# Reordering maxima, projections and the join of the maxima inside an attention group (order lists of one pipelined slot)

## The reference

```
q = split_heads(x @ Wq.T + bq); k = ...; v = ...
q_lr = einsum('bhtd,hdr->bhtr', q, Wq_lsr); k_lr = ...
scores = einsum('bhir,bhjr->bhij', q_lr, k_lr) * scale      # causal mask above the diagonal
attn = softmax(scores, axis=-1)
y = einsum('bhij,bhjd->bhid', attn, v);  out = y @ Wo.T + bo
```

## Time and profile before

| what | us |
|---|---|
| median of 3 runs | 4275.05 (4274.4 to 4277.15) |
| the profiled execution | 4274.05 |
| its span, first to last instruction | 4272.3 |
| PE matmul busy in the span | 3743.8 (88%) |
| DVE, ACT, POOL busy | 2262.9, 1473.4, 687.8 |

### The profile page before, as it was taken

How to read it: one execution, slowest core, us unless ns; L and a number is a source line. 1 busy time by engine, 2 the same in 40 slices (tenths; PEclk the granted TensorE clock), 3 DMA queues, 4 the chain that set the end, 5 groups by cost and what they waited for, 6 DMA issues and landing times. The chain is left out here.

```text
span 4272.3 us, 57451 instructions
## 1 busy us (share of the span) xinstructions
PE 3743.8 (88%) x21481; PEld 2587.1 (61%) x21481; DVE 2262.9 (53%) x3990; ACT 1473.4 (34%) x2753; POOL 687.8 (16%) x859
## 2 busy tenths in 40 slices
PE   5898998998998989989989832799999999999990
PEld 3555555555555555555555422788888888888880
DVE  2565564664664655655646457444454444544445
ACT  1343442443443433434424400333333333333324
POOL 2021121121121211211211210011111111111100
PEclk8999999999999999999999965699999999999995
DMA  4224233133322332242331110333344333443328
GB/s 154 68 81 113 58 102 98 46 97 98 93 70 78 100 102 64 79 117 59 102 97 41 43 57 5 104 117 106 121 127 136 114 108 121 126 136 113 111 69 324
DMA packets 187321, 422.56 MB, mean 99 GB/s; under 512 B 39777, under 2 KB 42849, under 8 KB 178401
## 3 DMA queue, kind: packets, MB, share of 16 engines
q1 hardware_dynamic: 167408, 367.98, 28.7%
q0 software_dynamic: 14336, 34.09, 4.2%
q10 hardware_dynamic: 5376, 17.83, 1.0%
HBM read 245.70 MB, written 72.38 MB: 74 GB/s over the span
## 5 line engine op out<-in xcount | busy, mean ns | idle before, releaser
L841 DVE TENSOR_REDUCE max_slots<-shared_banks 128x1 f32<-128x512 f32 (+3 forms) x1536 | 786.0, 548 | 497.0 <-PE shared_banks L636 370.7
L792 ACT ACTIVATE probs<-scores_t 128x512 f32<-128x512 f32 (+3 forms) x1536 | 671.4, 492 | 661.5 <-PE scores_t L678 653.1
L1510 PE MATMUL m_ps_h<-m_tokens_t,m_w_parts 128*128 128x512 f32 x3072 | 740.0, 391 | 1.6 <-DVE m_tokens_t L1448 1.6
L1510 PE MATMUL m_ps_y<-m_w_parts,m_hidden_parts 128*128 128x512 f32 x3072 | 737.0, 390 | 0.5
L678 PE MATMUL scores_t<-q_operands,k_operands 128*128 128x512 f32 (+3 forms) x1536 | 570.5, 412 | 114.3 <-DMA q_operands<-minus_max 108.3
L1510 PEld LDWEIGHTS m_ps_y<-m_w_parts,m_hidden_parts 128*128 128x128 f32 x3072 | 575.5, 188 | 125.3 <-issue 6.3
L1510 PEld LDWEIGHTS m_ps_h<-m_tokens_t,m_w_parts 128*128 128x128 f32 x3072 | 575.6, 188 | 120.1 <-issue 2.0
L633 PE MATMUL shared_banks<-k_operands,q_operands 96*128 96x512 f32 (+3 forms) x1536 | 555.0, 392 | 13.8 <-DVE natural L834 7.9
L1417 ACT ACTIVATE m_hidden<-m_ps_h,m_b 128x512 f32<-128x512 f32 x256 | 176.6, 690 | 817.8 <-PE m_ps_h L1510 804.6
L678 PEld LDWEIGHTS scores_t<-q_operands,k_operands 128*128 128x128 f32 x1536 | 294.0, 207 | 237.0 <-DMA q_operands<-minus_max 114.9
L633 PEld LDWEIGHTS shared_banks<-k_operands,q_operands 96*128 96x128 f32 x1536 | 314.5, 206 | 193.2 <-issue 138.2
(11 more groups left out here) (202 smaller groups left out, 3139.4 us busy)
## 6 DMA issues: line engine op xcount, KB each, us to landing
m_w_raw<-in_w1T SPq DMA_DIRECT2D x64, 1024.0 KB, 5.1
m_w_raw<-in_w2T SPq DMA_DIRECT2D x64, 1024.0 KB, 7.9
q_operands<-natural SPq DMA_DIRECT2D x384, 128.0 KB, 2.7
k_operands<-natural SPq DMA_DIRECT2D x384, 128.0 KB, 2.7
wqk_group<-scratch_wqk SPq DMA_DIRECT2D x32, 1024.0 KB, 5.2
natural<-in_xT SPq DMA_DIRECT2D x8, 2048.0 KB, 9.1
x_residual<-in_x SPq DMA_DIRECT2D x64, 256.0 KB, 2.7
scratch_x<-probs SPq DMA_DIRECT2D x64, 256.0 KB, 2.0
```

Of the source, the lines that this page charges most:

```text
L792: act.activation(probs[:, slot_of(k, h // 2), h % 2, c0:HALF], st[:, (HG * k + h) % SCORE_BANKS, c0:HALF], ACT.Exp, scale=SCALE).then_inc( ...
L841: dve.tensor_reduce(mx[:, h, slot:slot + 1], src[:, 0:n], AX.X, ALU.max).then_inc(bank_free[bank], 1)
L1510: mm = pe.matmul(bank, a, b, start=(first and n == 0), stop=(final and n == len(pairs) - 1))
```

## The change

Only the lists of the order change. The 48 maxima start behind part 8 instead of part 1 and end behind part 51 instead of part 55. Projections 0 and 1 stand at the parts 46 and 47 (before 47 and 49), projections 2 and 3 at 56 and 57 (before both at 50). The join stands at part 55 (before 58), so that projections 2 and 3 are behind it. The inversions of the first half move from 40, 44, 48, 49 to 30, 42, 45, 45; those of the second half of the group before, in the next slot, from 0, 0, 0, 14 to 0, 4, 4, 5. No instruction is added or taken away.

```diff
-MAX_AFTER = (0, 2, 2, 0, 1, 2, 0, 1, 2, 0, 2, 0, 1, 0, 1, 2, 0, 0, 0, 1,
-             0, 3, 1, 0, 1, 1, 1, 0, 1, 0, 2, 1, 1, 0, 1, 1, 1, 1, 1, 1,
-             0, 3, 0, 1, 0, 1, 1, 1, 1, 1, 0, 1, 1, 0, 1, 1, 0, 0, 0, 0)
-PROJ_AFTER = (47, 49, 50, 50)
-JOIN_AFTER = 58
-INVERT_AFTER = ((40, 44, 48, 49), (0, 0, 0, 14))
+MAX_AFTER = (0, 0, 0, 0, 0, 0, 0, 0, 2, 0, 2, 1, 1, 0, 3, 0, 0, 0, 3, 0,
+             2, 0, 3, 1, 0, 0, 2, 0, 1, 2, 0, 1, 2, 1, 2, 0, 0, 2, 1, 1,
+             0, 2, 2, 4, 1, 0, 1, 2, 1, 0, 1, 1, 0, 0, 0, 0, 0, 0, 0, 0)
+PROJ_AFTER = (46, 47, 56, 57)
+JOIN_AFTER = 55
+INVERT_AFTER = ((30, 42, 45, 45), (0, 4, 4, 5))
```

## The result

| | before | after |
|---|---|---|
| median of 4 runs, us | 4275.18 (4274.4 to 4277.15) | 4247.84 (4245.81 to 4250.01) |
| ratio to before, 95% interval | | 0.9935 [0.9918, 0.9953] |
| profiled span, us | 4272.3 | 4246.9 |
| mean granted clock of the span | 0.924 | 0.930 |

A forecast was written before the change was run, and what follows sets the result against it. PE's waits and clock bound the kernel; 103 + 41 - 35 - 13 - 13 - 36 - 13 - 11 - 7 = 16 us gained from 4274.05 gave 4258. Own range 4235 to 4267; 8 in 10: 4215 to 4310.

The forecast's parts named there:

- wait for the joined maxima: At starts of slots 1 to 3, PE's wait for the join's DMA, hidden by projections 2 and 3: 103 us gained.
- clock behind that wait: At 23 slots the granted clock no longer falls after the wait: 1.8 us each, 41 us gained.
- slot start without maxima: At 23 slot starts, only eight scores in parts 0 to 7, then strips: 1.5 us each, 35 us lost.
- x split, wait and clock: Slot 2, seven batches: PE waits 5.1 us for POOL's late split, 36 us lost; the clock falls, 13 us lost.
- tail and slot 0, with its clock, in batches 1 to 7: Late residual rows in seven tails lose 11 us; slot 0's maxima lose 13 over 8 batches, its fallen clock 13.
- DVE's lag: DVE's reductions, packed into fewer parts, fall behind: 0.3 us for 25 slots, 7 us lost.
- the undisturbed 52.65: Length in us of slot 0 before the change, at full clock, less a 0.52 us wait for an activation table.
- T: The moment PE leaves a slot's last weighing; times at the next slot's start are counted from it.
- the eight maxima: Maxima moved out of parts 0 to 7: done elsewhere they cost 1.7 us a slot, between 0.7 and 2.7.
- clock's rival: Clock falls at ordinary starts of slots 1 and 3 too: 2.5 us for 16 starts, 40 us, 4298; chance 0.30.
- cancelling rival: Maxima cost 2.7 and DVE lags 0.7 us a slot; half of that leaves 4275, no change; chance 0.21.
- hidden split: Slot 2's x split is in time after all: 36 + 13 us come back, with cheaper maxima 4187; chance 0.07.

The follow-up runs named there:

- experiment 2: Changed kernel's parts singly: join and projections with the old maxima order, 4353.83 us, 1.019; maxima and join with the old projections, 4269.66 us, 0.999.
- second kernel of experiment 2: Changed kernel with its maxima, join and inversions, but projections back at 47, 49, 50, 50: 4269.66 us, 0.999.
- experiment 1: POOL splits only 16 tokens of each chunk of the next x: on the changed kernel 4187.27 us, 0.9792; on the kernel before 4273.3 us, 0.9995.
- experiment 3: Changed kernel with slot 0's maxima from part 1, 4241.61 us; or slot 3's projections at 46, 47, 49, 50 and join at 58, 4238.95 us.
- experiment 5: Changed kernel, slot 2 rearranged, DVE subtracting one chunk of x, all projections behind the join: 4202.35 us; with slot 0 and slot 3 edits too, 4191.04 us.
- first kernel: Changed kernel with only slot 2 rearranged: DVE subtracts one chunk of x, inversions at 28 to 36, all projections behind the join: 4202.35 us, 0.983.
- second kernel of experiment 5: Changed kernel with slot 2 rearranged, slot 0's maxima from part 1 and slot 3's projections ahead of its last score: 4191.04 us, 0.9796.

## Why the prediction was right

The direction, the mechanism and the order of the terms held. By its own terms:

| term of the prediction | forecast | measured |
|---|---|---|
| wait for the joined maxima | +103 | +103, gone in all 24 slots |
| clock behind that wait | 23 x 1.8 = +41 | +41; clock 1.00 at all 23 starts |
| slot start without maxima | 23 x 1.5 = -35 | 23 x (53.84 - 52.65) = 23 x 1.2 = -28 |
| x split, wait and clock | 7 x (5.1 + 1.8) = -49 | 7 x (6.3 + 2.3) = -60 |
| tail and slot 0, with its clock, in batches 1 to 7 | -11 - 12 - 13 = -36 | -30 |
| DVE's lag | -7 | no wait seen |

The 41 can be checked in the kernel before: its 22 whole slots 1 to 3 last 54.5 us on average from first score to last weighing, 1.9 more than the undisturbed 52.65, 41 us in all. The last column gives 26, where the spans differ by 25. That it closes is no separate check, since the 28 and the 60 are what is left of whole slots. The forecast of 16 missed by less than its terms suggest: three terms were charged 6 to 7 us too high each, and the split 11 too low, so that a part of the closeness is luck.

One sum of the prediction does not come out. From the bounds of the slot start (23 us either way) and of DVE (7 less, 10 more) the range is 4228 to 4291; the 4267 stated lies 8.5 us under 4275, the least gain that a measurement can tell, and is no bound. The measured 4248 lies in either.

**The join.** The wait went in whole. In the last batch's slot 2, where I had let the joined maxima cost 1.4, PE waits 1.55 us, but for POOL's masks: it is the chain of experiment 2, which I had not seen, and that the two numbers agree is chance. In all slots with projections the projections cover that chain as well, so the sum doesn't show the gap; the second kernel of experiment 2 does, and there my estimate failed by 17 us and more.

**The slot start.** Step 0 was weighed at T + 3.5 (502.64 - 499.14) where 3.8 stood, and the first maximum came at T + 6.0 behind a wait of 0.55, where T + 6.2 and 0.5 stood. Its cost, 1.2 a slot, is what is left of slot 1 against the undisturbed 52.65 worked out from the earlier trace rows; the price of the eight maxima at their new places cannot be read apart from it. I had not foreseen that a few starts wait longer for strips: slot 3 of the batches 4 and 5 lasted 55.1 and 55.5 us, 1.3 and 1.7 more than the others.

**The next sequence's x.** This step was right and undersized: a wait of 6.3 on average, not 5.1. SP's queue and POOL, after the change, batch 1:

```profile
553.28 0.51 SPq L431 DMA_DIRECT2D q_operands<-natural  x1
...
571.09 0.39 SPq L413 DMA_DIRECT2D natural<-in_xT  x1
```

```profile
585.22 9.27 POOL L527 TENSOR_TENSOR x_parts<-natural,x_parts 128x1024 fp32r<-128x1024 f32 x4
```

T is 552.97 here. The strips start at T + 0.3 and not T - 0.2, and from them to the end of the split it is 594.49 - 553.28 = 41.2 us, not 40.1: these make the 6.62 of this slot out of 5.1. PE came to projection 0 at 594.63 - 6.62 = T + 35.0, as forecast (34.8). Wait and clock together, from slot 2's 62.4 against experiment 1's 53.8, are 8.6 a slot and not 6.9; less the 6.3 of the wait, 2.3 are left for the clock where 1.8 stood. That these 60 us are the split's and nothing else's, experiment 1 shows by taking the split's work away in both kernels.

**Slot 0 and the tail.** Slot 0's clock fell in five of the seven batches and not in all: 55.9 us where it fell, 54.5 where it held, 53.2 before. So the maxima cost 1.4, not 1.7, a fall cost 1.4, not 1.8, and I charged the falls too often. The tail's wait grew by 86.4 - 74.0 = 12.4 for the 11 forecast, and experiment 3 returns 10.5 of it by starting the strips earlier.

**The rivals.** The clock's rival is refuted at the place it named: the starts of slots 1 to 3 keep 1.00 with PE paced by ACT. Its premise, 1.7 us of work in 3.8, is not what the profile books: from 499.10 on PE counts as busy for 3.09 of 3.50 us (the ends of matmuls are modelled). The Trainium skill's page "TensorE: Matmul & The Clock Gate", section "A second HAM failure mode: psum-queue depth-cycling", says that brief pauses between groups of matmuls can swing the clock; at these starts they did not. The cancelling rival is refuted by its own condition, since the maxima cost the middle or less and DVE shows no lag: PE's weight loads wait 8.9 us for its reductions (L841) in place of 23.6 before. The hidden split did not come; the 4187 that I had given it is what the kernel took when the split was left out (4187.27). That agreement has luck in it, since terms on both sides were off by 6 to 11 us.

The waits of PE's weight loads for those reductions, after the change and before:

```profile
PEld shared_banks L633 <- DVE max_slots L841: 8.9, 41, 0.9
```

```profile
PEld shared_banks L633 <- DVE max_slots L841: 23.6, 69, 0.4
```

## What to carry to other kernels

When work is moved to hide one wait, list every chain that starts at the moved point, serial queues first: here the strips moved by 2.1 us (from 1.8 before the last weighing's end to 0.3 behind it), and three things behind them on one queue (the maxima, the next x, the tail's residuals) decided how much of the gain stayed. A filler of two matmul groups can cover several chains at once, so trying the parts of a reordering singly can show none of it (0.999 and 1.019) where the whole gains (0.9935). And where a stall has a single late producer, make a kernel without the producer's work first: its time shows what a real repair can bring (4187; the repair came to 4202).

## What the runs showed of the hardware

**Two engines that slow each other without a semaphore.** In experiment 5 DVE makes one low part of x (two SBUF inputs) beside POOL's. DVE and POOL, first kernel:

```profile
582.93 2.50 DVE L823 TENSOR_TENSOR x_parts<-natural,x_parts 128x1024 fp32r<-128x1024 f32 x1
...
586.86 1.55 DVE L857 COPY row_max<-max_slots 128x16 f32<-128x16 f32 x1
588.32 0.16 DVE L858 TENSOR_TENSOR row_max<-max_slots 128x16 f32<-128x16 f32 x1
```

```profile
578.91 0.76 POOL L541 TENSOR_SCALAR_AFFINE_SELECT probs<-probs 128x256 f32<-128x256 f32 x2
579.64 4.70 POOL L531 TENSOR_TENSOR x_parts<-natural,x_parts 128x1024 fp32r<-128x1024 f32 x2
584.30 1.75 POOL L541 TENSOR_SCALAR_AFFINE_SELECT probs<-probs 128x256 f32<-128x256 f32 x2
586.02 2.35 POOL L531 TENSOR_TENSOR x_parts<-natural,x_parts 128x1024 fp32r<-128x1024 f32 x1
```

The same subtraction took 1.22 us each in the lead-in of the changed kernel (4.63 for four, overlapping a little), where POOL ran fills alone (MEMSET). Here it takes 2.50 and ends (585.43) 1.1 us after POOL's pair of subtractions (584.34), about as if it had begun then. So it is in all seven batches: it took 1.95 to 3.18 us and ended 1.08 or 1.09 us behind POOL's pair. POOL pays too: its two masks from 584.30 on take 1.75 us, where the two before the pair take 0.76. The copy of 128x16 values, as small as the 0.16 us operation behind it, takes 1.55 and ends (588.41) with POOL's subtraction (588.37). That also holds in all seven batches (1.55 to 1.56 us), while none of the trace's other 25 such copies took more than 0.43. The join's last wait of 0.57 us is behind that copy. In the second kernel of experiment 5 the profiled execution shows the longest case, in batch 1:

```profile
580.46 6.60 DVE L827 TENSOR_TENSOR x_parts<-natural,x_parts 128x1024 fp32r<-128x1024 f32 x1
```

POOL's subtractions and masks followed one another there until 585.98, and DVE's subtraction ended 1.08 us later; PE then waited 3.96 us at the join. The Trainium skill, page "SBUF — State Buffer", section "Who interferes with whom", states that DVE shares a pair of ports with POOL which is an exclusive lock, that a DVE instruction with two SBUF inputs contends for it with a POOL instruction that reads SBUF, and that a copy can do so in its two-port modes. These ends agree with it. No run here was made to test it.

**What the clock forgave.** PE with 3.09 us of work in 3.50, in short pauses, kept 1.00 (499.1). PE with 1.99 in 3.60 kept it in one batch (741.4), and much the same start lost it in another (443.3). What decides between the last two stays open. Behind a wait of 6.6 us PE was still at 0.51 on average over the next 6.4 us (594.6 to 601.0).
